# Moving VectorE's residual sum of the previous visit between the bias and the gate of the next one in a one-core attention and mixture-of-experts kernel

## The reference, cut to what matters

```python
assignments = jnp.argmax(logits, axis=-1)
weights = jnp.take_along_axis(softmax(logits), assignments[:, None], axis=1)[:, 0]
hid = gelu(einsum('nd,edf->nef', x, w1) + b1)
all_out = einsum('nef,efd->ned', hid, w2) + b2
sel = all_out of the assigned expert
x = x + gb * (sel * weights[:, None])
```

## Time and profile before

| what | value |
|---|---|
| three runs, median | 618.04 us |
| three runs, lowest to highest | 617.46 to 618.93 us |
| the profiled execution's own time | 615.35 us |
| its span | 613.5 us |
| granted TensorE clock, mean over the span | 0.639 |
| expert stage, VectorE's first to last bias | 501.3 to 603.6 us |

### The profile page before, as it was taken

How to read it: one execution, slowest core, us unless ns; L and a number is a source line. 1 busy time by engine, 2 the same in 40 slices (tenths; PEclk the granted TensorE clock), 3 DMA queues, 4 the chain that set the end, 5 groups by cost and what they waited for, 6 DMA issues and landing times.

```text
span 613.5 us, 11885 instructions
## 1 busy us (share of the span) xinstructions
PE 474.6 (77%) x2537; PEld 267.5 (44%) x2537; DVE 563.2 (92%) x1432; ACT 542.3 (88%) x2310; POOL 483.0 (79%) x642
## 2 busy tenths in 40 slices
PE   5457887877887788788778778878776777988992
PEld 2113433333443333344334334434333356878982
DVE  5898999999999999999999999999999887988984
ACT  2599999999999999999999999999999945766761
POOL 4566777999989899898998999898898755767653
PEclk9555556566556655655665655555665587999997
DMA  6365544445555545555545555655655116976750
GB/s 193 106 186 156 137 139 124 138 141 151 146 148 147 149 144 155 166 143 159 153 141 151 142 144 150 173 171 143 172 147 164 70 56 199 307 232 196 226 167 22
DMA packets 77071, 94.41 MB, mean 154 GB/s; under 512 B 12806, under 2 KB 60710, under 8 KB 76998
## 3 DMA queue, kind: packets, MB, share of 16 engines
q1 hardware_dynamic: 68842, 75.69, 44.6%
q0 software_dynamic: 6144, 16.82, 7.3%
q10 hardware_dynamic: 2015, 1.15, 0.7%
HBM read 58.41 MB, written 35.20 MB: 153 GB/s over the span
## 4 chain that ended last, share of the span: by engine, by line
ACT 70%; PE 11%; DVE 10%; issue 4%; DMA 2%; ACTq 1%; POOL 1%; DVEq 0%; SPq 0%; POOLq 0%
ACT scores L910 69%; PE scores L1199 4%; PE scores L1190 4%; DVE neg_max L1362 3%; PE scores L1182 1%; DMA table<-rows,place_i 1%; DVE y_biased_s L1933 1%; DVE packed L1956 1%; DVE bn L1291 1%; DMA x_s<-table 1%; ACTq L574 0%; DMA k_stack<-parts_dram 0%; DMA parts_dram<-parts 0%; DVE w_ring L1928 0%; ACT exp_l L923 0%
## 5 line engine op out<-in xcount | busy, mean ns | idle before, releaser
L910 ACT ACTIVATE scores<-scores,neg_max 128x256 f32<-128x256 f32 x1024 | 467.7, 847 | 10.6 <-DVE neg_max L1362 10.5
L910 ACT ACTIVATION_READ_ACCUMULATOR scores<-scores,neg_max 128x1 f32 x1024 | 436.9, 608 | 0.0
L1362 DVE TENSOR_REDUCE neg_max<-scores 128x4 f32<-128x1024 f32 x256 | 309.2, 1211 | 8.1 <-PE scores L1042 7.6
L1042 PE MATMUL scores<-k_stack,q_stack 64*128 64x256 bf16 x1024 | 149.3, 391 | 77.2 <-ACT scores L910 64.6
L1042 PEld LDWEIGHTS scores<-k_stack,q_stack 64*128 64x128 bf16 x1024 | 34.1, 106 | 161.7 <-ACT scores L910 116.2
L823 POOL DMA_INDIRECT table<-rows,place_i x64 | 66.0, 1031 | 18.9 <-issue 16.7
L876 POOL DMA_INDIRECT out_dram<-out_room,x_s x51 | 49.7, 975 | 22.6 <-DVE out_room L1946 11.7
L1199 PE MATMUL scores<-w_s,hid 128*128 x308 | 51.5, 291 | 4.7 <-ACT hid L942 2.2
L772 POOL TENSOR_SCALAR xhat<-rows,mv,rstd 128x128 f32<-128x128 f32 x60 | 47.6, 794 | 7.1 <-POOL rstd L755 7.1
L1070 PE MATMUL side_a<-w_gated,opt_t 128*128 128x128 f32 x128 | 50.3, 496 | 0.0
L764 POOL TENSOR_SCALAR xhat<-x_s,mv,rstd 128x128 f32<-128x128 f32 x62 | 49.0, 799 | 0.4 <-POOL rstd L755 0.4
(11 more groups left out here) (224 smaller groups left out, 883.2 us busy)
## 6 DMA issues: line engine op xcount, KB each, us to landing
x_s<-table SPq DMA_DIRECT2D x77, 192.5 KB, 3.1
q_stack<-parts_dram SPq DMA_DIRECT2D x192, 64.0 KB, 2.9
parts_dram<-parts SPq DMA_DIRECT2D x31, 384.0 KB
k_stack<-parts_dram SPq DMA_DIRECT2D x186, 64.0 KB, 2.3
mod_b<-mod_rows SPq DMA_DIRECT2D x32, 256.0 KB, 4.4
x_s<-in_x_dram SPq DMA_DIRECT2D x13, 256.0 KB, 4.8
table<-pad_tile SPq DMA_DIRECT2D x15, 192.5 KB
w1x_s<-in_w1x_dram SPq DMA_DIRECT2D x7, 258.0 KB, 4.6
```

The costliest lines, as they stand in the source:

```text
L910: last = act.activation(buf[:, k * L:k * L + L], buf[:, k * L:k * L + L], ACT.Exp, bias=neg_max[:, p, n:n + 1], accum_out=exp_sum[:, p, n: ...
L1042: last = pe.matmul(scores[:, c, at:at + L], q_stack[p][r, g + j, t * P:t * P + P], k_stack[p][r, g + j, :], start=True, stop=True)
L1362: dve.tensor_reduce(to, scores[:, (PAIRS * b.n + i) % RING, :].rearrange("p (e j m) -> p e j m", e=2, j=2), AX_X, ALU.max, negate=True).th ...
```

## The change

In a turn of VectorE from turn 5 on, the residual sum of the previous visit is done between the bias and the gate of the current one, and no longer behind the gate. The merge stays last. No instruction is added or dropped, and each keeps its operands and its semaphores.

```diff
                 elif n > PRIMED:
                     if in_range(n):
                         bias_y(n)
-                        gate_y(n)
                     if n > PRIMED + 1:
                         out_y(n - 1)
+                    if in_range(n):
+                        gate_y(n)
                     if shared_of_visit(n - 2) is not None:
                         merge(n - 2)
```

## The result

| | before | changed |
|---|---|---|
| median, same chip | 617.93 us (4 runs) | 611.41 us (4 runs) |
| lowest to highest | 617.46 to 618.93 us | 610.86 to 612.07 us |
| profiled execution, own time | 615.35 us | 611.94 us |
| its span | 613.5 us | 610.1 us |

The changed kernel takes 0.9893 of the time before, with a 95% interval of 0.9875 to 0.9911: 6.5 us less. The forecast was 612.0 us, a gain of 6.0. The three gains are 6.5, 5.0 and 3.3 us between medians, 4.9 on average. The sign is safe, and the size lies at 3 to 7 us.

A forecast was written before the change was run, and what follows sets the result against it. VectorE was taken to set the pace in planning, mixed and last visits, TensorE in whole visits about 27 to 44. 7.3 + 0.1 - 0.85 - 0.4 - 0.1 = 6.0 us gained, so 612.0 us; range 610.4 to 616.2.

The forecast's parts named there:

- The cost of the wait: VectorE, bias to gate: the gate's wait removed saves 0.11 us a turn, over 66 turns 7.3 us.
- The residual sum behind the bias: VectorE: the moved residual sum waits for nothing and starts 0.20 to 0.21 us behind the bias; bounds 0.20 and 0.32.
- nothing comes free: Rival at VectorE's bias: whatever follows it is held until it ends, gain 0, time 618.0 us; chance 0.11.
- TensorE as the bound: Whole visits up to visit 46: VectorE can only close up to TensorE's 1.01 us turn; 0.8 to 0.9 us lost.
- the brakes that act on single turns: Single turns in the first thirty where TensorE's pace shows through: 0.1 us lost.
- the cap of 3.1: At visit 46: VectorE's shift is at most about 3.1 us, where 36 turns would have given 4.0.
- The row slots: Visit 48's load waits for visit 32's store, paced by GpSimd; 0.3 to 0.4 us lost, bounds 0 and 1.5.
- My limit of 1.5 us: Sign on TensorE's waits for loaded rows: a sum over 1.5 us makes the forecast wrong.
- the row loop takes more: Rival: GpSimd's stores bound 546 to 568 us and rows land late; gain 2 to 4.5, about 614.8 us; chance 0.15.
- The later part: Turns after visit 46: average 1.12 us becomes 1.01, last turns 1.19 become 1.08; that shift gets through.
- The clock: TensorE, 523 to 598 us: below 1.00 refutes the forecast; rival: each low-clock turn loses 0.9 us, slower from seven; chance 0.07.
- The sum: Whole kernel: the gain minus the losses is 6.0 us, giving 612.0 us.

The follow-up runs named there:

- gate_last: Changed kernel with the gate also moved behind the merge (bias, residual sum, merge, gate); 613.75 us, ratio to before 0.9935.
- gate_other: Order of before, but from visit 5 the gate multiplies the previous visit's biased result, using third buffers; 611.02 us, ratio to before 0.9893.
- serial_out: Order of before, but the residual sum takes the visit whose gate stands right ahead, a second wait; 627.33 us, ratio to before 1.0165.
- after_again: The changed kernel measured and profiled a second time, with no edit; 613.01 us, ratio to before 0.9931.
- half_stores: Changed kernel without GpSimd's stores of every second whole visit from 7 on, their slots freed after the residual sum; 612.73 us, ratio to before 0.9922.
- after_third: The changed kernel measured and profiled a third time, with no edit; 613.03 us, ratio to before 0.9931.
- early_only: Kernel before, with the changed order only in visits 5 to 44 and the old order from visit 45; ratio to before 0.9968.
- fills_late: Changed kernel with the last eight table fills behind the loads of visits 22 to 36 instead of 16 to 30; 613.33 us, ratio to before 0.9938.
- busy_reload: Changed kernel with four unused matmuls ahead of TensorE's register loads at visits 28, 38, 50 and 67; 612.65 us, ratio to before 0.9928.
- short_residual: Changed kernel with the residual sum of whole visits from 5 on cut to 16 of 128 columns; 611.83 us, ratio to before 0.9907.

## Why the prediction was right, point by point

- **The cost of the wait** is shown from both sides. 0.32 became 0.20, by reordering (the changed kernel, gate_last) and by another operand (gate_other), and a second wait costs the same again (serial_out). I had 0.11 a turn; the timelines give 0.12, and 66 turns 7.9 us and not 7.3.
- **The residual sum behind the bias** starts 0.20 later, the lower of the two bounds. With that "nothing comes free" is refuted, and so is, for this pair, the rule of the Trainium skill, "VectorE: DVE Perf Modes", section "The DRAIN you can't avoid", that I had set against it. The trace agrees with a later section of that page of the Trainium skill, "Two Vector instructions with no wait between them", by which an instruction is held only on certain conditions, such as inputs that start in other groups of partitions; all operations here start in partition 0.
- **TensorE as the bound** came as described: in the changed profile the turns up to the biases of visits 31, 32, 39 and 40 take 1.00 or 1.01 us, TensorE's own pace. But the shift at visit 46 was forecast at 3.1 less 0.1, and its bias is earlier by only 1.4, 1.7 and 1.9 us in the three profiles, taken from the bias of visit 10. I counted TensorE at its own pace as the only brake in this half, and put the brakes that act on single turns at 0.1: this is the term that was mis-sized. Another 1.1 to 1.7 us went. What the profiles show in this half are late rows at changing visits (1.68 us at 536.22 in after_again) and the one fall of the clock. half_stores, where no row is late behind 523 us and the clock stays at 1.00, has the bias of visit 46 earlier by 3.2 us: there the cap of 3.1 came out, which supports it and puts the loss on what that profile lacks. It is one profile.
- **The row slots** were mis-sized too: 0.3 to 0.4 at visit 48 against waits of 1.8, 3.1 and 3.9 us in all (1.0 before), over the whole stage and not near visit 48 alone (in the first changed profile at 520.71, 523.11, 570.11 and 584.89 us). My limit of 1.5 us is passed in every profile of the changed kernel, so by that sign of my own this step was wrong. The rival "the row loop takes more" was right in its mechanism: the waits grew by 0.8 to 2.9 us. Its time, a gain of 2 to 4.5, fits one of the three measured gains (3.3), my forecast's 4.5 to 7.4 the other two (6.5 and 5.0). The store of visit 25, which I had near 544.9, started at 547.59, late by the hole and the fall of the clock at visit 28 and by the later start of the stage. Taken from the bias of visit 10 it came earlier by 0.4, 0.9 and 0.3 us in the three profiles, where 1.9 was forecast. In after_third neither hole nor clock explains that: there the stores follow each other 1.26 to 1.40 us apart from visit 20 on, GpSimd's own pace, and that of visit 25 starts 4.3 us behind its bias where it was 3.1. I had let them wait for VectorE up to visit 25.
- **The later part** paid more than forecast: from visit 63 on 0.15 a turn, 1.95 instead of 1.4 us. Of it 1.6 are 13 steps of 0.12; the other 0.4 are a weight copy that held the next operation for 0.39 us instead of 0.20 and two gates with 0.29 behind them instead of 0.21, which the profile of before has there and the changed one has not. early_only, with the old order in this part, again takes 14.69, so they seem to belong to the old order; why was not tried.
- **The clock.** I had written that anything below 1.00 between 523 and 598 would make the forecast wrong. It did fall, in one profile of three, for about 4 us, and with its hole cost 1.0 to 1.4 us, yet the kernel was faster all the same, so that condition was too strict. The rival's mechanism is real at a fraction of its price: it needed a fall of seven turns, and none so long was seen.
- **The sum** landed well in part by luck, because its misses offset each other and the first measurement was the most favourable of three (6.5 us, then 5.0 and 3.3). In the profiles 0.6 us more came from the turns and 0.4 more at the end, against 1.8 to 3.3 us more lost, in which late rows and holes have their part; from the bias of visit 10 to that of 76 they show 4.5, 5.1 and 3.6 us less, and not 6.0. And the medians differ by more than the profiles, since the execution profiled of before was 2.6 us faster than its median while the changed one was not (611.94 beside 611.41). I had carried these 2.7 over to the changed kernel. Where the median execution of before spends them is not visible in any profile here.

## What to carry to other kernels

Read an engine's timeline by starts: where a step is longer than the others (0.32 among 0.20) and the operation waits for the one right ahead of it, an independent operation put between them takes the step away, without a single instruction less. Then ask at once what is next: here some 5 of the 7.9 us came through, as TensorE and the loads of rows stood close behind (with half of the stores left out, 7.2 did in the same turns). And put no single execution's profile against another's for differences of 1%: the same kernel gave 75.2 to 76.7 us for the same 66 turns.

## What the runs showed of the hardware beyond what was expected

- A hole of TensorE is followed by the lower clock in some executions and not in others. It fell behind 1.50 (changed, first profile), 1.64 (gate_other, clock 0.72 from 541 to 547 us) and 2.07 us (fills_late), and stayed at 1.00 behind 1.68 (after_again), 1.84 (busy_reload), 1.48 (short_residual) and 1.30 us (half_stores). The length of the hole alone doesn't decide.
- The same register load of TensorE at visit 28 left holes of 0.5 to 1.6 us from one profile to the next, of closely related kernels (0.7, 0.9 and 1.5 in the three of the changed kernel), and of 0.56 and 0.27 us where matmuls were queued ahead of it.
- Late rows come at other visits in each of the three profiles of the changed program, and its timed runs spread over 5.7 us (609.98 to 615.65 in the three measurements), those of before over 3.6 (615.35 to 618.93).
- GpSimd's closing instruction, behind its last store, took 10.0 us in half_stores and 7.4 before and after the change: with fewer stores the end of the program was longer.
